# GpSimd's part of a graph layer written out without a loop: gathers with fixed index columns, no bounds check on them, no copies of the indices

## What is computed

```python
deg = jnp.maximum(jax.ops.segment_sum(jnp.ones(dst.shape), dst, num_segments=100000), 1.0)
norm = (deg ** -0.5)[:, None]
h = jnp.maximum(_layernorm(x), 0.0)
h_src, h_dst = h[src], h[dst]
msg = (h_src @ W1 + h_src * h_dst @ W2) * (norm[src] * norm[dst])
h_N = jax.ops.segment_sum(msg, dst, num_segments=N) + h @ W1
g = jnp.where(h_N >= 0, h_N, 0.2 * h_N)
out = x + g / jnp.maximum(jnp.sqrt(jnp.sum(g * g, axis=1, keepdims=True)), 1e-12)
```

## Time and profile before

| what | value |
|---|---|
| time, median of 3 runs | 988.85 us |
| lowest and highest | 986.76 and 989.3 us |
| span of the profiled execution | 992.8 us |
| busy: PE, DVE, ACT, POOL | 75%, 87%, 71%, 79% |
| instructions of POOL | 694 |
| mean granted TensorE clock | 0.903 |
| bytes moved by DMA | 172.89 MB, mean 174 GB/s |

### The profile page before, as it was taken

The page is one execution under the profiler, slowest core; times in us unless marked ns, Lnnn a source line. Parts: engine busy times, 40 slices in busy tenths (PEclk is TensorE's granted clock), DMA queues, the critical chain, the costliest instruction groups (busy, mean ns, idle before and its releaser), DMA issues.

```text
span 992.8 us, 21320 instructions
## 1 busy us (share of the span) xinstructions
PE 746.4 (75%) x6104; PEld 720.4 (73%) x6104; DVE 859.6 (87%) x2731; ACT 704.7 (71%) x2944; POOL 779.8 (79%) x694
## 2 busy tenths in 40 slices
PE   1499787878887876887788788688776887788830
PEld 1399787877877876787787788678776887778830
DVE  6689999999998888889799998888788888888980
ACT  0088878888787776677687878767686677677960
POOL 2788888878888888888888888888888888887672
PEclk9999999999999987789999989878888798798975
DMA  3814564656556545564465564456445654564531
GB/s 86 271 49 153 169 234 145 238 169 209 199 161 204 189 147 166 180 216 157 154 231 186 187 219 156 146 192 219 150 149 171 209 185 152 188 208 154 179 131 59
DMA packets 68803, 172.89 MB, mean 174 GB/s; under 512 B 14383, under 2 KB 34514, under 8 KB 62434
## 3 DMA queue, kind: packets, MB, share of 16 engines
q1 hardware_dynamic: 49868, 135.41, 40.3%
q0 software_dynamic: 18816, 36.08, 11.5%
HBM read 96.89 MB, written 77.04 MB: 175 GB/s over the span
## 4 chain that ended last, share of the span: by engine, by line
POOL 67%; issue 19%; DVE 7%; ACT 3%; POOLq 1%; PE 1%; DMA 0%; SPq 0%; DVEq 0%; ACTq 0%
POOL xd L461 24%; POOL xs L461 24%; POOL out L466 16%; DVE xo L820 2%; DVE bst L780 1%; POOL sstage L477 1%; POOL stage L472 1%; ACT junk L933 1%; DVE oe L812 1%; DVE cjk L752 0%; DVE agg L840 0%; ACT hd L925 0%; DVE ybuf L865 0%; DMA out<-oe,sstage 0%; ACT junk L964 0%
## 5 line engine op out<-in xcount | busy, mean ns | idle before, releaser
L461 POOL DMA_INDIRECT xs<-in_x,stage x196 | 267.9, 1367 | 53.3 <-issue 53.3
L461 POOL DMA_INDIRECT xd<-in_x,stage x196 | 258.1, 1317 | 59.7 <-issue 59.7
L1066 PE MATMUL pt<-nident,bst 128*128 128x128 f32 x1568 | 303.2, 297 | 0.0
L1076 PE MATMUL pu<-w,ct 128*128 128x128 f32 x1568 | 221.1, 292 | 67.6 <-ACT ct L917 67.6
L1066 PEld LDWEIGHTS pt<-nident,bst 128*128 128x128 f32 x1568 | 267.6, 214 | 0.0
L466 POOL DMA_INDIRECT out<-oe,sstage x196 | 220.5, 1125 | 59.8 <-issue 58.7
L1076 PEld LDWEIGHTS pu<-w,ct 128*128 128x128 f32 x1568 | 201.4, 204 | 76.3 <-ACT ct L917 76.2
L1063 PE MATMUL pt<-ident,xin 128*128 128x128 f32 x784 | 232.5, 297 | 8.5 <-DVE bst L780 5.3
L933 ACT ACTIVATE junk<-ybuf 128x128 bf16<-128x128 f32 x784 | 234.0, 308 | 0.0
L820 DVE SCALAR_TENSOR_TENSOR xo<-ybuf,rd,xin 128x128 f32<-128x128 f32 x784 | 210.0, 344 | 0.0
L933 ACT ACTIVATION_READ_ACCUMULATOR junk<-ybuf 128x1 f32 x784 | 156.3, 199 | 0.0
(11 more groups left out here) (136 smaller groups left out, 1255.5 us busy)
## 6 DMA issues: line engine op xcount, KB each, us to landing
xin<-in_x SPq DMA_DIRECT2D x96, 512.0 KB, 4.8
out<-xo SPq DMA_DIRECT2D x48, 1024.0 KB
srow<-src_rows SPq DMA_DIRECT2D x49, 256.0 KB, 6.8
edge_rows<-oe SPq DMA_DIRECT2D x49, 256.0 KB
same<-same_segment SPq DMA_DIRECT2D x49, 128.0 KB, 6.2
xs<-in_x,stage POOLq DMA_INDIRECT x196, 2.9
xd<-in_x,stage POOLq DMA_INDIRECT x196, 7.1
out<-oe,sstage POOLq DMA_INDIRECT x196
```

What stands on the lines that cost most here:

```text
L461: pool.indirect_dma_start(out=to, out_offset=None, in_=rows, in_offset=bass.IndirectOffsetOnAxis(ap=index, axis=0), bounds_check=limit, oo ...
L1066: last = pe.matmul(pt[:, q % 2, f], mean[:, s.buf(0, 2), col:col + 1].to_broadcast([P, D]), nident[:], start=False, stop=True)
L1076: last = pe.matmul(pu[:, q % 2, f], ct[:, q % 2, f], w1[:], start=True, stop=True)
```

## The change

POOL's part for gathers and scatters is written as plain Python loops over all 49 steps, so that each step has its own instructions and no register counts steps; the helper `steps` with its hardware loop is no longer used there. The other engines keep theirs. `stage_gather` and `stage_scatter` go, with their tensors and semaphores, and each DMA takes its index column from `idx` itself at a fixed place. The gathers have no `bounds_check`; the scatters keep it. The waits for the other engines and for earlier DMAs are the same counts at the same places (in `gather_rows` they now stand before the first gather of the step, as they did in the text before).

```diff
-            def gather(to, rows, index, limit, done):
-                pool.indirect_dma_start(out=to, out_offset=None, in_=rows,
-                                        in_offset=bass.IndirectOffsetOnAxis(ap=index, axis=0),
-                                        bounds_check=limit, oob_is_err=False).then_inc(done, 16)
+            def gather(to, index, done):
+                pool.indirect_dma_start(out=to, out_offset=None, in_=x,
+                                        in_offset=bass.IndirectOffsetOnAxis(ap=index, axis=0)).then_inc(done, 16)
...
-            def stage_gather(s, d):
-
-                pool.tensor_copy(stage[:, s.buf(d, XBUFS), :],
-                                 idx[:, bass.ds(s(d), 1), 0:2, :, :].rearrange("p o a q h -> p (o a q h)")
-                                 ).then_inc(staged, 1)
...
-                pool.wait_ge(staged, s(d + 1))
-                if has(i, d + 1):
-                    stage_gather(s, d + 1)
+            def row_index(i, a, k):
+
+                return idx[:, i, a, k // 2, k % 2:k % 2 + 1]
+
+            def gather_rows(i):
+
+                s, b = Step(0, i), i % XBUFS
+                if i >= XBUFS:
+                    pool.wait_ge(relu_done, s(1 - XBUFS))
+                    pool.wait_ge(f_done, s(1 - XBUFS))
+                after = i - XBUFS + 1
+                if after >= 0:
+                    pool.wait_ge(xs_got[after % XBUFS], (after // XBUFS + 1) * 16 * TE)
+                    pool.wait_ge(xd_got[after % XBUFS], (after // XBUFS + 1) * 16 * TE)
                 for k in range(TE):
-                    gather(xs[:, b, k, :], x, stage[:, b, k:k + 1], row_limit, xs_got[b])
+                    gather(xs[:, b, k, :], row_index(i, 0, k), xs_got[b])
                 for k in range(TE):
-                    gather(xd[:, b, k, :], x, stage[:, b, TE + k:TE + k + 1], row_limit, xd_got[b])
...
-                    pool.wait_ge(sstaged, s(-2))
-                    if has(i, -2):
-                        stage_scatter(s, -2)
                     for k in range(TE):
-                        scatter(oe[:, b, k, :], sstage[:, b, k:k + 1], scattered[b])
-
-            steps(pool, do, STEPS + 2)
+                    scatter(oe[:, b, k, :], row_index(i, 2, k), scattered[b])
+
+            for i in range(STEPS + 3):
+                if i == 0:
+                    for early in range(AHEAD):
+                        gather_rows(early)
+                if i + AHEAD < STEPS:
+                    gather_rows(i + AHEAD)
+                if i >= 3:
+                    scatter_rows(i - 3)
```

## The result

The changed kernel takes 994.35 us (median of 12 runs, 985.75 to 1001.17), the kernel before beside it 987.81 us (12 runs, 980.04 to 999.03). By these medians it is 0.7% slower. An execution can fall in a slower state, so every ratio with an interval here compares only the executions within 1.5% of the fastest of the same kernel; this one is 1.0103 (1.006 to 1.0147). So the kernel did not become faster, and a loss of 0.7 to 1% is little beside the 1.6 to 1.9% by which the executions of either kernel differ among themselves. The forecast was 962 us with a range of 915 to 990; the time lies 4 us above the range and on the other side. The profiled execution spans 999.5 us. It is the longest of the twelve (1001.17 us), and the one of before (992.8 us) lies above its median too, so what is counted in the two traces holds for one execution of each.

What follows compares the result with a forecast made beforehand. POOL's queue of 588 indirect DMAs was taken as the bound. Copies 10 us plus check 20 us, less 2 to 3 us lost early, left 27 us off 988.85: 962 us, range 915 to 990.

Steps and rivals of the forecast that it cites:

- the first rival: In late steps POOL no longer holds VectorE, which sets the pace: 914 to 925 us; chance 0.22 for 914 to 940.
- The check: Bounds check on POOL's 392 gathers: removal saves 0.05 us each, 20 us in all, ends 0 and 78 us.
- The gap between a step's last gather and its first scatter: Sign on POOL's queue: with the copy gone this gap should be 0.30 us.
- The copies: Two index copies a step on POOL: removal saves 0.2 us a step, 10 us over 49 steps.
- The 13 us that I counted at nothing: Copies' hold-ups behind VectorE: the next DMA would be held to the same moment; otherwise up to 13 us more gain.
- Loop and index column: POOL's loop branches and reading `idx` in place of `stage`: removal or replacement changes nothing that shows, 0 us each.
- it is on the path in nearly all steps: POOL's queue: its 30 us saving counts in nearly all steps, less 2 to 3 us lost in a few early ones.
- the busy time of the three DMA groups beyond their undisturbed durations should stay near 160 us: Sign on POOL's DMAs: hold-ups unchanged by the change; under 100 us would mean VectorE is the bound.
- the second rival: POOL's saved time lies before VectorE instructions that hold it to a fixed moment: 983 to 987 us; chance 0.11.
- Its reason against: Against the saving being taken back: the same DMAs must be caught, yet starts move by 0.07 to 0.5 us.
- The late step: Sign in the late stretch: L820 to L820 should take near 19.0 us, against 19.64 us before.
- The slower rival: Without the copy gathers start earlier against L820 and the wrong one is held: up to 1011 us; chance 0.15 for 989 to 1011.

Runs made afterwards that it cites:

- `breaks`: Changed kernel with three one-column VectorE memsets among the 16 instructions of L820: 923.89 us, ratio 0.9282 to the kernel before.
- `check_back`: Changed kernel with the gathers' bounds check put back, no index copies and no loop: 967.98 us, ratio 0.9815 to the kernel before.
- `loop_away`: Kernel before with POOL's loop written out and columns fixed, index copies and bounds check kept: 994.72 us, ratio 1.0128.
- The pads: Changed kernel with one-column POOL memsets ahead of first, fourth, fourth and fifth gathers, or first scatter, in seven variants: 990.38 to 1001.73 us.
- `copies_back`: Changed kernel with the two index copies a step put back, gathers still without bounds check: median 969.53 us, runs from 928 to 982.

## Why the prediction was wrong

**The bound.** That POOL sets the late steps and VectorE the early ones holds, before and after: 73% of the chain is POOL's, and `breaks` shows that 7% of the time is to be had as soon as POOL is held less. (The waits before L812 were read as 16.3 us; with the wait put down to the DMA they are 20.0 us, which changes nothing in this.) What `breaks` shows is the first rival's mechanism ("VectorE becomes the bound", 914 to 925 us), at the time it gave: 923.89 us. But it was reached by the breaks, and the change alone does not bring it about.

**The prices.** The check was put at 0.05 us a gather; it is 0.055 (1.00 to 0.945), 22 us of POOL's queue. The gap between a step's last gather and its first scatter is 0.30 us, as said. The copies were put at 10 us, with up to 13 more if their own hold-ups vanish. `check_back` against `before` is 18 to 21 us, by ratio and by medians, with 161 us of hold-ups left in the DMAs as before: it is more than 10 us, but the term need not be too small. The 13 us that I counted at nothing did for the most part pass to the next DMA, as said: the hold-ups of DMAs started in L865 are 60.7 us in `check_back` and 63.1 in the changed kernel against 46.9 before. In `check_back` those behind L820 fell beside it, to 78.4 us from 92.9. Loop and index column were put at 0. `loop_away` says 0.6 to 1.9% slower by its ratio, 0.6% by its medians, and its trace has nothing to show for it. That part is not settled.

**The step that failed** is "it is on the path in nearly all steps", together with "the busy time of the three DMA groups beyond their undisturbed durations should stay near 160 us". In a late step of the circle above the eight gathers are not on the path: they lie beside L820 and L865 and wait for their ends. What the runs showed in place of the saving of 27 us is a median circle step of 19.51 us against 19.63, and hold-ups of 220 us. That was the second rival, "the hold-ups take the saving back", 983 to 987, with a chance of 0.11. Its reason against (that the same DMAs must be caught) did not weigh: it is enough that some DMA is caught, and in 48 of 49 steps one is. The late step became 19.5 us, not 19.0. The pads bear it out: up to 11 us of work more ahead of the gathers did not make the kernel slower than the changed one.

**Why slower, not only equal.** This is shown less well, since the loss is under 1%. The hold-ups rose from 162 us (175 with the copies') to 220 us. The slower rival named the place (L820) and the kind of cause (another gather is caught), but with the third gather for the fourth, 4.41 for 3.11 us. What is seen is that escapes vanish: 36 of L820's runs held a DMA before, 48 do now (44 to 49 in the seven kernels with pads), and long steps begin earlier. Taken in isolation, neither the check nor the copies does this (33, 20 and 33 runs that hold). Why their joint removal does is not explained by the place of the start, and none of the seven pads broke it. Shown are the hold-up, its price and that a break ends it; why the two removals together meet more hold-ups than either alone is not.

**The chances.** I gave 0.12 to slower and called the catching of DMAs the weak spot of any forecast, but built the range from one carried-over sum of 162 us. Nothing in the trace of before fixed that sum; it ran with `copies_back` at 119 us and with the changed kernel at 220 us, and 100 us of hold-ups on the bound engine is 10% of the time.

## What to carry to other kernels

Before counting the saving of shorter instructions on the engine that sets the end, walk once round the period of a late step and sum only what stands between one release and the next: here only 0.12 us of what the change removed was in the sum. Where long DMAs of GpSimd end at a fixed distance behind a run of two-input VectorE instructions, put a break into the run first (three one-column memsets gave 6 to 7% in both kernels), and judge other changes after that. A kernel whose runs differ by several per cent with the same instructions (928 to 982 us in `copies_back`, 922.6 to 924.3 with breaks) may have such hold-ups in its path; the spread is a reason to look for them, not a proof.

## What the runs showed of the hardware

A bounds check costs an indirect gather of 128 rows 0.055 us (1.00 against 0.945 us). A one-column memset of GpSimd hides in the 0.30 us pause ahead of an indirect DMA: one adds 0.02 us, three 0.03, six 0.11 and ten 0.23. A GpSimd DMA that is started within a back-to-back run of VectorE instructions with two SBUF inputs each may be held, mostly until 0.82 us after the run's end (0.87 with a bounds check), so that it takes up to 5.0 us, or not at all; with three breaks of 0.06 us in the run none of 176 was held, while the single instruction L865 of 2.29 us went on holding 44 of 46. From a last scatter's end to the start of the VectorE instruction that waits for it are 1.32 us.
